# Probabilities of batch 0 turned by a trip through HBM and VectorE's block transpose, with attention three tiles behind the scores

## The chip, the cores and the metric

The kernel runs on one core of a Trainium2 chip. The metric is the device time of one launch in microseconds. TensorE is called PE in the profile, VectorE DVE, ScalarE ACT, GpSimd POOL, and SyncE, which issues most DMAs, SP. Each engine takes its instructions in order; semaphores order engines among each other.

## The reference

Two batches of 1024 tokens, width 512, all in float32.

```python
xn = layernorm(x)                                  # x: (2, 1024, 512)
q, k, v = split(xn @ w_qkv.T + b_qkv)
probs = softmax(q @ k.T / sqrt(512))               # one head, 1024 x 1024 for a batch
s = (probs @ v) @ w_out.T + b_out
logits = xn @ router_w + router_b                  # 8 experts
top2 of logits, weights = softmax(top2)
comb = sum over the top 2 of weight * silu(xn @ expert_w[e] + expert_b[e])
y = xn + comb @ proj_w + proj_b
out = x + s * silu(norm_w * y / rms(y))
```

## The kernel before

**Precision and folding.** Every product of two float32 matrices is made as three matmuls (function `product`, L1449): a value is split into a high half, as ScalarE casts it, and a low half, the difference, made by VectorE or GpSimd. Output weights are folded into the values and query weights into the keys, so that a query tile's attention is: scores (`scores`, 24 matmuls), row maximum, exp, turn of the probabilities, product with the values (`attend`, 24 matmuls), division and bias (`attn_out`).

**Stages.** Weights are folded; both batches are normalised, and their rows go to HBM (`rows_scratch`); values of batch 0; logits; then attention of batch 0, during which VectorE also works out the routing (`choose`, a generator whose steps stand between the other work), GpSimd sends every token's row into its expert's slots in HBM by indirect DMA, and ScalarE and GpSimd split expert weights; then 39 tiles of expert work; values, attention, projection and output of batch 1 and the output of batch 0.

**Attention of batch 0.** Eight tiles of 128 queries against 1024 keys, in two blocks of four. At the head of a block TensorE makes four key products (`key_weights`, 12 matmuls each), whose halves (`t_hi` on ScalarE, `t_lo` on VectorE) are the stationary side of the scores. Key products, value products, attention products and expert products share the two banks of the PSUM tensor `ab` in the order of the list `U`; each waits until the entry two before it is read (`ab_read`). Scores go to two pairs of banks (`sc`), and `scores` of a tile waits for exp of the tile two before it. `tp`, two banks, takes what is turned.

For each tile VectorE finds the maximum (`row_max`, L1245 to L1249) and ScalarE makes exp into `prob`, a single 128x1024 buffer. TensorE turns it by eight 128x128 transposes into `tp` (`turn_probs`, L1457), ScalarE copies the high half (`pt_split`, L906), VectorE the low half (`pt_low`, L1264), and TensorE makes the product. Order on TensorE in a block: scores 0 and 1, turn 0, scores 2, turn 1, product 0, scores 3, turn 2, product 1, turn 3, product 2, product 3.

**Around it.** SyncE stores each result tile of attention (L533), loads rows to be sent (L496), and, as the last tiles pass, raw weights of experts 3 and 4 (`load_raw`), biases, and the rows of the first expert tiles (`load_pair`, L502: four DMAs that bring quarters of 128 rows to 32 partitions each). VectorE turns those rows in blocks of 32x32 (`turn`, L1237), and ScalarE and VectorE split them (`g_split`, `g_low`). GpSimd loads six raw weights through two halves of a buffer (`BY_BUFFER`); ScalarE makes high halves (`early_high`, `w_high`), GpSimd low halves. The first expert tile waits for the halves of four experts (`EARLY`) and for both attention banks.

```python
                for j in range(QB):
                    if j >= 1:
                        pt_split(j - 1)
                    if (i, j) in EARLY_AT:
                        early_high(EARLY_AT.index((i, j)))
```

## Time and profile before

| | us |
|---|---|
| median of 3 runs (507.84 to 508.83) | 508.24 |
| the profiled execution | 505.39 |
| its span, first to last instruction | 503.7 |
| TensorE busy | 488.0 |
| VectorE busy | 299.7 |
| ScalarE busy | 206.7 |
| GpSimd busy | 202.6 |

The profile is of one execution. A row of a timeline has the start from the span's begin, the duration, the engine, the source line and the operation with output and inputs; in brackets stands how long the engine had been idle and what ended that. A slice of the page is 12.6 us; its digit is the busy share in tenths. Matmuls are pipelined, so their records overlap.

### The profile page before, as it was taken

Reading aid. Unit: us, or ns where it says so; the run is one execution under the profiler, and the core shown is the slowest. Engines: PE = TensorE matmul, PEld = TensorE weight load, DVE = VectorE, ACT = ScalarE, POOL = GpSimd, SP = SyncE. Lnnn points to the kernel's source line nnn. Section 1 sums busy time; section 2 is a strip of 40 time slices with the busy share of each in tenths; the row PEclk is TensorE's granted clock in tenths of the full one; section 3 lists DMA queues with packets and bytes.
Section 4 is the critical chain, followed back from the end, with each engine's and each line's share of the span. In section 5 each row is a group of like instructions: output and inputs, shape, how many; then the busy total and the mean of one; then the engine's idle time right before and its main releaser. Section 6 shows DMA issues by size and latency. Waiting matters only on the chain.

```text
span 503.7 us, 7293 instructions
## 1 busy us (share of the span) xinstructions
PE 488.0 (97%) x2234; PEld 397.2 (79%) x2235; DVE 299.7 (60%) x452; ACT 206.7 (41%) x300; POOL 202.6 (40%) x288
## 2 busy tenths in 40 slices
PE   4999999999999999799999999999999999999996
PEld 2678686888888888688888888878888888888884
DVE  2556252576422535688888889763676645667452
ACT  1166373142212333854444444323454362525550
POOL 3044310004887835860000000754477772466134
PEclk9999999999999999999999999999999999999999
DMA  7863999912688489998985666987253451331202
GB/s 261 303 231 145 379 384 366 394 43 84 220 310 298 159 248 285 307 272 247 287 219 189 188 202 181 311 287 276 65 148 114 150 175 62 116 95 62 84 33 94
DMA packets 68364, 104.22 MB, mean 207 GB/s; under 512 B 5728, under 2 KB 29808, under 8 KB 68336
## 3 DMA queue, kind: packets, MB, share of 16 engines
q1 hardware_dynamic: 55120, 67.13, 42.1%
q0 software_dynamic: 7360, 25.19, 14.6%
q10 hardware_dynamic: 5856, 11.54, 6.5%
q8 instruction: 16, 0.26, 0.2%
q14 instruction: 12, 0.10, 0.1%
HBM read 60.32 MB, written 43.52 MB: 206 GB/s over the span
## 4 chain that ended last, share of the span: by engine, by line
PE 90%; DMA 3%; issue 2%; ACT 2%; POOL 1%; DVE 1%; SPq 1%; ACTq 0%
PE ab L1451 20%; PE ab L1453 20%; PE ab L1452 20%; PE sc L1451 6%; PE sc L1453 6%; PE sc L1452 6%; PE tp L1457 4%; PE sc L1468 3%; DMA raw<-in_expert_w 2%; PE tp L1502 2%; DMA raw_o<-in_w_out_t 1%; PE sc L1531 1%; PE ab L1476 1%; ACT W L941 1%; PE sc L1534 1%
## 5 line engine op out<-in xcount | busy, mean ns | idle before, releaser
L720 POOL DMA_INDIRECT y<-y_scratch,pos x32 | 31.1, 972 | 107.2 <-DMA y_scratch<-yt_so 92.5
L1451 PE MATMUL ab<-W,st_h 128*128 x156 | 60.9, 390 | 2.7 <-DVE st_l L1189 2.7
L1453 PE MATMUL ab<-W,st_l 128*128 x156 | 60.7, 389 | 0.0
L1452 PE MATMUL ab<-W,st_h 128*128 x156 | 60.7, 389 | 0.0
L703 POOL DMA_INDIRECT rows_scratch<-xb,pos x32 | 31.2, 976 | 52.4 <-DVEq L1185 44.2
L1451 PE MATMUL sc<-xt_h,t_h 128*128 128x512 f32 x128 | 50.3, 393 | 0.0
L1453 PE MATMUL sc<-xt_h,t_l 128*128 128x512 f32 x128 | 50.0, 390 | 0.0
L1452 PE MATMUL sc<-xt_l,t_h 128*128 128x512 f32 x128 | 49.8, 389 | 0.0
L932 ACT CAST st_h<-tp 128x512 fp32r<-128x512 f32 x39 | 22.9, 588 | 42.8 <-PE ab L1453 34.1
L1245 DVE TENSOR_REDUCE small<-sc 128x1 f32<-128x1024 f32 x16 | 19.6, 1224 | 29.8 <-PE sc L1453 25.4
L1451 PEld LDWEIGHTS ab<-W,st_h 128*128 128x128 f32 x156 | 29.3, 188 | 9.6 <-issue 3.5
L1453 PEld LDWEIGHTS ab<-W,st_l 128*128 128x128 f32 x156 | 29.3, 188 | 6.1
L1452 PEld LDWEIGHTS ab<-W,st_h 128*128 128x128 f32 x156 | 29.3, 188 | 5.9
L1082 DVE SCALAR_TENSOR_TENSOR t_l<-ab,tb,t_h 128x512 fp32r<-128x512 f32 x16 | 12.0, 750 | 34.3 <-ACT t_h L832 34.3
L1189 DVE TENSOR_TENSOR st_l<-tp,st_h 128x512 fp32r<-128x512 f32 x39 | 26.5, 681 | 4.5 <-ACT st_h L932 4.4
L832 ACT ACTIVATE t_h<-ab,tb 128x512 fp32r<-128x512 f32 x16 | 11.0, 690 | 42.5 <-PE ab L1453 40.4
L1237 DVE STREAM_TRANSPOSE tp<-xn 128x512 f32<-128x512 f32 x24 | 26.3, 1098 | 3.3 <-DMA xn<-rows_scratch 1.0
L1453 PEld LDWEIGHTS sc<-xt_h,t_l 128*128 128x128 f32 x128 | 24.0, 188 | 5.0
L1452 PEld LDWEIGHTS sc<-xt_l,t_h 128*128 128x128 f32 x128 | 24.0, 188 | 4.9
L1451 PEld LDWEIGHTS sc<-xt_h,t_h 128*128 128x128 f32 x128 | 24.0, 188 | 4.8
L1237 DVE STREAM_TRANSPOSE tp<-xg 128x512 f32<-128x512 f32 x23 | 25.1, 1097 | 2.2
L1451 PE MATMUL ab<-v_h,p_h 128*128 128x512 f32 x64 | 25.6, 400 | 0.0
(261 smaller groups left out, 1219.0 us busy)
## 6 DMA issues: line engine op xcount, KB each, us to landing
rows_scratch<-xn ACTq DMA_DIRECT2D x3, 3328.0 KB, 19.3
xb<-in_expert_w POOLq DMA_DIRECT2D x6, 1024.0 KB
xn<-rows_scratch SPq DMA_DIRECT2D x48, 128.0 KB, 3.0
xg<-rows_scratch SPq DMA_DIRECT2D x44, 128.0 KB
y_scratch<-yt_own SPq DMA_DIRECT2D x20, 256.0 KB, 2.6
y_scratch<-yt_so SPq DMA_DIRECT2D x19, 256.0 KB, 2.8
rows_scratch<-xs SPq DMA_DIRECT2D x16, 256.0 KB, 6.0
xb<-rows_scratch SPq DMA_DIRECT2D x16, 256.0 KB, 6.2
```

The costliest lines, as they stand in the source:

```text
L703: pool.indirect_dma_start(slots_d, bass.IndirectOffsetOnAxis(pos[:, g:g + 1], 0), sent_rows[:, g % GB, :], None).then_inc(sent[g % GB], 16)
L720: pool.indirect_dma_start(y[:, q, :], None, y_d, bass.IndirectOffsetOnAxis(pos[:, GB * s + p:GB * s + p + 1], 0))\
L932: nc.scalar.copy(st_h[:, h, :, :], tp[:, h, :, :]).then_inc(g_hi, 1)
L1082: vec.scalar_tensor_tensor(low[:, n, :], bank(("t", b, i, n)), tb[:, n:n + 1], high[:, n, :], ALU.add, ALU.subtract).then_inc(ab_read, 1)
L1189: vec.tensor_tensor(st_l[:, h, :, :], tp[:, h, :, :], st_h[:, h, :, :], ALU.subtract).then_inc(g_lo, 1)
L1237: vec.transpose(tp[:, q % 2, :, :].rearrange("p c (r s) -> p c r s", r=4), rows[q].rearrange("p (r q c) -> p c r q", r=4, c=KC)).then_inc( ...
L1245: link(vec.tensor_reduce(small[:, at, 0:1], sc[:, n % 2, :, :], AX.XY, ALU.max, negate=True))
L1451: nc.tensor.matmul(dst, lh, rh, start=start, stop=False)
L1452: nc.tensor.matmul(dst, lh, rl, start=False, stop=False)
L1453: return nc.tensor.matmul(dst, ll, rh, start=False, stop=stop)
L1457: last = nc.tensor.transpose(tp[:, h, c, :], src[:, c * P:(c + 1) * P], ident[:, :])
L1468: last = nc.tensor.matmul(sc[:, n // 2, n % 2, :], every_fourth(raw[2][:, c, :], n), raw[3][:, c, :], start=(c == 0), stop=(c == KC - 1))
```

## The change

The turn of batch 0's probabilities leaves TensorE. Exp writes a tile with its columns in another order, so that the row falls into four quarters of 256 values. SyncE stores the tile to HBM (`p_scratch`, 512 KB) and reads it back by four DMAs of 128 KB; in the way back quarter a of all 128 rows lands in partitions 32a to 32a+31. Two block transposes on VectorE (`p_turn`) then give what the eight transposes of TensorE gave. Three tile buffers (`prob`, and `xn` or `yt_own`) hold what is being stored, and the two halves of `xs` what came back.

The two blocks become one run of eight tiles, and the product with the values follows its scores three tiles behind. The second set of key products stands behind scores 3 and product 0. The orders of SyncE, ScalarE and VectorE are written out anew; in the routing, positions now come before the table of experts (`texp`), with a semaphore for each (`routed`, `assigned`). Raw weights 3 come through the buffer on GpSimd's queue, and raw weights 6 by a DMA of ScalarE in a place of their own.

```diff
-    BY_BUFFER = EARLY + (5, 6)
+    BY_BUFFER = EARLY + (3, 5)
...
+    p_d = nc.dram_tensor("p_scratch", (GB, P, S), F32).ap()
+    p_q = p_d.rearrange("j (r s) (a f) -> j a s r f", r=4, a=4)
...
-              + [u for i in range(NB) for u in [("t", 0, i, n) for n in range(KC)]
-                 + [("a", 0, QB * i + j) for j in range(QB)]]
+              + [("t", 0, 0, n) for n in range(KC)] + [("a", 0, 0)]
+              + [("t", 0, 1, n) for n in range(KC)] + [("a", 0, j) for j in range(1, GB)]
...
+        xn_flat = xn[:, :, :].rearrange("p a n -> p (a n)")
+        yt_flat = yt_own[:, :, :].rearrange("p a n -> p (a n)")
+        probs = tuple(prob[:, :] if j % 2 == 0 else xn_flat if j < QB else yt_flat for j in range(GB))
+        quarters = tuple(xs[:, 2 * n:2 * n + 2, :].rearrange("p a n -> p (a n)") for n in range(2))
...
-            sb("experts_0_to_2", [P, 3, 2, KC, D], F32R, a)
-            sb("expert_3_high", [P, KC, D], F32R, a)
-            raw_3 = sb("raw_3", [P, KC, D], F32, a)
+            sb("experts_0_to_3", [P, 4, 2, KC, D], F32R, a)
             sb("expert_4_high", [P, KC, D], F32R, a)
             raw_4 = sb("raw_4", [P, KC, D], F32, a)
-            sb("experts_5_to_7", [P, 3, 2, KC, D], F32R, a)
+            sb("expert_5", [P, 2, KC, D], F32R, a)
+            sb("expert_6_high", [P, KC, D], F32R, a)
+            raw_6 = sb("raw_6", [P, KC, D], F32, a)
...
-            for j in range(GB):
-                if j == QB + 1:
-                    sp.wait_ge(s_done, GB)
-                    load_raw(sp, 3)
-                    load_bias(0)
-                    load_bias(1)
-                if j == QB + 2:
-                    sp.wait_ge(ptr_done, 1 + GB)
-                    load_pair(2, 1)
-                    load_raw(sp, 4)
-                    load_next(4, 0)
-                    load_bias(2)
-                    load_bias(3)
...
+            def store_prob(j):
+                sp.wait_ge(exp_done, 2 + j + 1)
+                sp.dma_start(p_d[j], probs[j], max_dma_last_dim=4 * D).then_inc(p_out[j % 2], 16)
+            def load_prob(j):
+                sp.wait_ge(p_out[j % 2], 16 * (j // 2 + 1))
+                if j >= 2:
+                    sp.wait_ge(p_turned, j - 1)
+                for a in range(4):
+                    sp.dma_start(quarters[j % 2][32 * a:32 * (a + 1), :].rearrange("p (r f) -> p r f", r=4),
+                                 p_q[j, a, :, :, :]).then_inc(p_in[j % 2], 16)
+            def store_s(j):
                 sp.wait_ge(ab_read, 2 + U["a", 0, j] + 1)
                 sp.dma_start(s_g[j], so[:, j % 2, :]).then_inc(so_st[j % 2], 16)
-                if 1 <= j <= 3:
-                    for g in range(GB + 3 * j - 3, min(GB + 3 * j, G)):
-                        load_to_send(g)
-                if j == QB:
-                    for g in range(GB):
-                        sp.wait_ge(sent[g], 64)
-                    load_pair(0, 0)
-                if j == QB + 3:
-                    load_next(6, 1)
-                    for k in range(4, E):
-                        load_bias(k)
+            sp.wait_ge(t_done, G)
+            for j in range(QB):
+                store_prob(j)
+                load_prob(j)
+            store_s(0)
+            for g in range(GB, GB + 4):
+                load_to_send(g)
+            for j in (QB, QB + 1):
+                store_prob(j)
+                load_prob(j)
+                store_s(j - 3)
+                for g in range(GB + 4 + 2 * (j - QB), GB + 6 + 2 * (j - QB)):
+                    load_to_send(g)
+            store_prob(GB - 2)
+            load_prob(GB - 2)
+            store_s(3)
+            store_prob(GB - 1)
+            load_prob(GB - 1)
+            sp.wait_ge(s_done, GB)
+            load_raw(sp, 4)
+            for g in range(GB):
+                sp.wait_ge(sent[g], 64)
+            load_pair(0, 0)
+            store_s(4)
+            load_pair(2, 1)
+            load_bias(0)
+            load_bias(1)
+            store_s(5)
+            load_next(4, 0)
+            load_bias(2)
+            load_bias(3)
+            store_s(6)
+            store_s(7)
+            load_next(6, 1)
...
-                    act.wait_ge(routed, 1)
+                    act.wait_ge(assigned, 1)
...
-            def attention_block(i):
-                for c in range(KC):
-                    if i or c:
-                        t_hi(0, i, c)
-                def pt_split(j):
-                    act.wait_ge(ptr_done, 1 + QB * i + j + 1)
-                    nc.scalar.copy(pt_h[:, j % 2, :, :], tp[:, :, :, :].rearrange("p a c n -> p (a c) n"))\
-                        .then_inc(pt_hi, 1)
-                for j in range(QB):
-                    if j >= 1:
-                        pt_split(j - 1)
-                    if (i, j) in EARLY_AT:
-                        early_high(EARLY_AT.index((i, j)))
-                    act.wait_ge(mx, QB * i + j + 1)
-                    act.wait_ge(ptr_done, QB * i + j + 1)
-                    nc.scalar.activation(prob[:, :], sc[:, j % 2, :, :].rearrange("p a n -> p (a n)"), ACT.Exp,
-                                         bias=small[:, 4 + j, 1:2], scale=SCALE,
-                                         accum_out=small[:, 4 + j, 2:3]).then_inc(exp_done, 1)
-                    if i == 0 and j == 0:
-                        act.wait_ge(gate_d, 1)
-                        nc.scalar.activation(small[:, 10, :], small[:, 9, :], ACT.Exp).then_inc(gate_e, 1)
-                pt_split(QB - 1)
...
+            def pt_split(j):
+                act.wait_ge(p_turned, j + 1)
+                if j >= 2:
+                    act.wait_ge(ab_full, U["a", 0, j - 2] + 1)
+                nc.scalar.copy(pt_h[:, j % 2, :, :], tp[:, :, :, :].rearrange("p a c n -> p (a c) n")).then_inc(pt_hi, 1)
+            def exp_0(j):
+                act.wait_ge(mx, j + 1)
+                if j >= 2:
+                    act.wait_ge(p_out[j % 2], 16 * (j // 2))
+                nc.scalar.activation(probs[j].rearrange("p (a c q) -> p c a q", a=4, q=32),
+                                     sc[:, j % 2, :, :].rearrange("p m (c a q) -> p (m c) a q", a=4, q=32), ACT.Exp,
+                                     bias=small[:, 4 + j % QB, 1:2], scale=SCALE,
+                                     accum_out=small[:, 4 + j % QB, 2:3]).then_inc(exp_done, 1)
+            for n in range(1, KC):
+                t_hi(0, 0, n)
+            exp_0(0)
+            act.wait_ge(gate_d, 1)
+            nc.scalar.activation(small[:, 10, :], small[:, 9, :], ACT.Exp).then_inc(gate_e, 1)
+            act.wait_ge(zero_in, 48)
+            exp_0(1)
+            early_high(0)
+            pt_split(0)
+            exp_0(2)
+            exp_0(3)
+            pt_split(1)
+            pt_split(2)
+            for n in range(KC):
+                t_hi(0, 1, n)
+            early_high(1)
+            exp_0(4)
+            pt_split(3)
+            exp_0(5)
+            early_high(2)
+            pt_split(4)
+            exp_0(6)
+            pt_split(5)
+            exp_0(7)
+            pt_split(6)
+            early_high(3)
+            act.wait_ge(s_done, GB)
+            w_high(0)
+            w_high(1)
+            pt_split(7)
...
+            w_high(2)
+            w_high(3)
...
-            load_raw(act, E)
+            load_raw(act, 6)
...
-                row_max(QB * i)
-                go_on()
-                row_max(QB * i + 1)
-                go_on()
-                pt_low(0)
-                row_max(QB * i + 2)
-                go_on()
-                pt_low(1)
-                go_on()
-                attn_out(0)
-                row_max(QB * i + 3)
-                pt_low(2)
-                attn_out(1)
-                pt_low(3)
-                if tail:
-                    dve.wait_ge(pt_lo, 1 + GB)
-                    turn(0, 0, 0, True)
-                    turn(1, 1, 0, True)
-                    g_low(0, 0)
-                    g_low(1, 1)
-                attn_out(2)
-                attn_out(3)
-                if tail:
-                    turn(2, 2, 0)
-                    turn(3, 3, 0)
...
+            def p_turn(j):
+                dve.wait_ge(p_in[j % 2], 64 * (j // 2 + 1))
+                dve.wait_ge(pt_lo, j)
+                back = quarters[j % 2].rearrange("p (r c q) -> p c r q", r=4, q=32)
+                for h in range(2):
+                    last = vec.transpose(tp[:, h, :, :].rearrange("p c (r s) -> p c r s", r=4),
+                                         back[:, h * KC:(h + 1) * KC, :, :])
+                last.then_inc(p_turned, 1)
...
+            routing = choose()
+            for n in range(KC):
+                t_lo(0, 0, n)
+                if n == 2:
+                    read_logits()
+            next(routing)
+            row_max(0)
+            next(routing)
+            row_max(1)
+            next(routing)
+            p_turn(0)
+            row_max(2)
+            pt_low(0)
+            next(routing)
+            next(routing, None)
+            row_max(3)
+            p_turn(1)
+            pt_low(1)
+            p_turn(2)
+            attn_out(0)
+            pt_low(2)
+            p_turn(3)
+            for n in range(KC):
+                t_lo(0, 1, n)
+            for j in range(3, GB - 1):
+                row_max(j + 1)
+                attn_out(j - 2)
+                pt_low(j)
+                p_turn(j + 1)
+            attn_out(GB - 3)
+            pt_low(GB - 1)
+            dve.wait_ge(pt_lo, GB)
+            turn(0, 0, 0, True)
+            turn(1, 1, 0, True)
+            g_low(0, 0)
+            g_low(1, 1)
+            attn_out(GB - 2)
+            attn_out(GB - 1)
+            turn(2, 2, 0)
+            turn(3, 3, 0)
...
-                def turn_probs(j):
-                    a = QB * i + j
-                    pe.wait_ge(exp_done, a + 3)
-                    pe.wait_ge(pt_lo, a + 1)
-                    transpose_tile(prob[:, 0:KC * P], 0)
-                    transpose_tile(prob[:, KC * P:2 * KC * P], 1).then_inc(ptr_done, 1)
-                def attend_tile(j):
-                    pe.wait_ge(pt_lo, QB * i + j + 2)
-                    attend(0, QB * i + j, pt_h[:, j % 2, :, :], pt_l[:, j % 2, :, :], v_h, v_l)
-                if not route_here:
-                    for n in range(KC):
-                        key_weights(0, i, n)
-                scores(0, QB * i)
-                if route_here:
-                    count_chosen()
-                scores(0, QB * i + 1)
-                pe.wait_ge(lg_read, 1)
-                if route_here:
-                    pe.wait_ge(cnt_read, 1)
-                turn_probs(0)
-                scores(0, QB * i + 2)
-                turn_probs(1)
-                attend_tile(0)
-                scores(0, QB * i + 3)
-                turn_probs(2)
-                attend_tile(1)
-                turn_probs(3)
-                attend_tile(2)
-                attend_tile(3)
...
+            def attend_tile(j):
+                pe.wait_ge(pt_lo, j + 1)
+                attend(0, j, pt_h[:, j % 2, :, :], pt_l[:, j % 2, :, :], v_h, v_l)
+            scores(0, 0)
+            count_chosen()
+            for j in range(1, QB):
+                scores(0, j)
+            attend_tile(0)
+            for n in range(KC):
+                key_weights(0, 1, n)
+            for j in range(QB, GB):
+                scores(0, j)
+                attend_tile(j - 3)
+            for j in range(GB - 3, GB):
+                attend_tile(j)
...
-            pe.wait_ge(routed, 1)
+            pe.wait_ge(assigned, 1)
```

`w_high` is as before and only moved up; `pt_low` and `attn_out` are as before but for their index.

## Rows read from the trace of the kernel before

**Rows 1.** The page: busy time by engine, DMA share and rate by slice

```profile
PE 488.0 (97%) x2234; PEld 397.2 (79%) x2235; DVE 299.7 (60%) x452; ACT 206.7 (41%) x300; POOL 202.6 (40%) x288
...
DMA  7863999912688489998985666987253451331202
GB/s 261 303 231 145 379 384 366 394 43 84 220 310 298 159 248 285 307 272 247 287 219 189 188 202 181 311 287 276 65 148 114 150 175 62 116 95 62 84 33 94
```

**Rows 2.** Timeline of PE at the first expert tiles (start us, us, what)

```profile
199.85 0.39 PE L1451 MATMUL ab<-W,st_h 128*128 x1
...
205.07 0.39 PE L1453 MATMUL ab<-W,st_l 128*128 x1
207.80 0.49 PE L1451 MATMUL ab<-W,st_h 128*128 x1 [2.35 <-DVE st_l L1189]
...
211.17 0.49 PE L1451 MATMUL ab<-W,st_h 128*128 x1 [0.36 <-DVE st_l L1189]
```

**Rows 3.** Timeline of PE, scores of tile 1 and the transposes behind them

```profile
99.95 0.48 PE L1451 MATMUL sc<-xt_h,t_h 128*128 128x512 f32 x1
...
105.51 1.04 PE L1457 MATMUL tp<-ident,prob 128*128 128x128 f32 x8
```

**Rows 4.** The chain that ended last, the same eight transposes

```profile
105.68 0.88 PE tp L1457 x8
```

**Rows 5.** Timeline of DVE, two block transposes of expert rows and two low halves

```profile
191.43 2.06 DVE L1237 STREAM_TRANSPOSE tp<-xn 128x512 f32<-128x512 f32 x2
193.40 1.44 DVE L1189 TENSOR_TENSOR st_l<-tp,st_h 128x512 fp32r<-128x512 f32 x2
```

**Rows 6.** Timeline of DVE in the attention of batch 0

```profile
100.25 1.22 DVE L1245 TENSOR_REDUCE small<-sc 128x1 f32<-128x1024 f32 x1
...
105.79 1.22 DVE L1245 TENSOR_REDUCE small<-sc 128x1 f32<-128x1024 f32 x1 [1.45 <-PE sc L1453]
...
107.37 0.17 DVE L1152 COPY w<-small 128x16 f32<-128x16 f32 x1
...
109.73 1.23 DVE L1264 TENSOR_TENSOR pt_l<-tp,pt_h 128x1024 fp32r<-128x1024 f32 x1
...
113.66 0.47 DVE L1171 TENSOR_TENSOR slots<-slot_i,small 128x312 f32<-128x312 f32 x1
...
114.90 1.23 DVE L1264 TENSOR_TENSOR pt_l<-tp,pt_h 128x1024 fp32r<-128x1024 f32 x1
116.04 0.28 DVE L1178 SCALAR_TENSOR_TENSOR route<-small,route 128x128 f32<-128x128 f32 x1
...
118.51 0.17 DVE L1270 RECIPROCAL small<-small 128x1 f32<-128x1 f32 x1 [0.15 <-PE ab L1453]
118.71 0.75 DVE L1272 SCALAR_TENSOR_TENSOR so<-ab,small,sbias 128x512 f32<-128x512 f32 x1
```

**Rows 7.** Timeline of ACT, attention and first expert tiles

```profile
102.96 0.19 ACT L917 ACTIVATION_READ_ACCUMULATOR prob<-sc,small 128x1 f32 x1
...
106.59 1.01 ACT L906 CAST pt_h<-tp 128x1024 fp32r<-128x1024 f32 x1 [3.33 <-PE tp L1457]
...
192.61 0.59 ACT L932 CAST st_h<-tp 128x512 fp32r<-128x512 f32 x1 [2.47 <-DVE tp L1237]
...
194.01 2.00 ACT L941 CAST W<-raw 128x1024 fp32r<-128x1024 f32 x2
```

**Rows 8.** Stores of expert outputs (L548, 256 KB each), 225 to 300 us

```profile
DMA to landing us min/median/max: 2.0/2.6/4.5
```

**Rows 9.** Loads of expert rows (L502, 128 KB each), 225 to 300 us

```profile
DMA to landing us min/median/max: 2.4/2.7/4.5
```

**Rows 10.** Timeline of SyncE's queue, four loads of expert rows

```profile
217.14 1.82 SPq L502 DMA_DIRECT2D xg<-rows_scratch  x4
```

**Rows 11.** DMA issues, 128 to 140 us (size each, us to landing)

```profile
xb<-rows_scratch SPq DMA_DIRECT2D x4, 256.0 KB, 4.1
```

**Rows 12.** DMA issues of the whole span, the raw expert weights

```profile
raw<-in_expert_w SPq DMA_DIRECT2D x2, 1024.0 KB, 9.3
```

88 lines of the change are left out of this document (37 added, 51 removed).

## The prediction

> **What bounds the kernel now.** The page's busy line comes first: TensorE (PE) is busy in 97% of the span [rows 1], so what TensorE sheds is worth its full time as long as nothing takes its place, and every stall put on it costs in full. The DMA and GB/s lines under it say where the queues are full: digits 1 and 2 from 101 to 126 us, 6 to 8 up to 164, 4 up to 176, 8 or 9 behind that. PE's timeline shows how the matmuls follow each other: 24 of them (one tile's scores, or one tile's attention product) from 199.85 take 5.45 us, 0.227 each [rows 2]. The records are 0.39 long because they overlap; the distance between starts is what counts. The same rows hold the only idle PE between the start of batch 0's attention and the end of the experts: 2.35 and 0.36 us at the third and fourth expert tile, both ended by st_l. The fourth starts at 211.17; three tiles back (12 matmuls, 2.72 us each) that is 203.0. A kernel whose expert tiles ran without a gap would equal this one if its first started at 203.0, not 199.85. I use that as the mark.
>
> **Removed.** Eight 128x128 transposes for each of 8 tiles. PE's timeline has a group of eight at 105.51 [rows 3]; the chain that ended last charges such a group 0.88 us [rows 4]. Eight groups are 7.1 us. All of it lies on the bound, so with no new wait the first expert tile would start at 199.85 - 7.1 = 192.75.
>
> **Added on VectorE.** Two block transposes for a tile. The trace has the operation in the same form into the same PSUM tensor: two take 2.06 us, about 2.0 up to the next [rows 5]; 8 tiles are 16 us on an engine that has room on average (60%). But its queue is in order, and where a turn stands in it decides. The transposed copy waits for data out of HBM, and row_max of the next tile stands behind it.
>
> **Early: VectorE's queue.** Only rows of before, and the new order. Scores 1 start at 99.95 [rows 3] and scores 3 end at 116.4 (three tiles, the first 0.1 longer, no transposes). VectorE's durations up to its next operation, from [rows 6]: row_max 1.58; routing step three 2.36; the low half of the probabilities 1.14; slots and texp 1.24; positions 2.47; attn_out 0.95. From row_max's start to the end of exp, with its read of the sum, are 2.9 us (100.25 to 103.15 [rows 6, 7]). The turn of tile 0 needs its round trip through HBM: exp 0 ends at 103.15, and with 7.5 us for the trip (below) the quarters are there at 110.7. From there: turn 0 to 112.7, row_max 2 to 114.3, low half 0 to 115.45 (so the attention product of tile 0 starts at 116.4 unhindered), positions to 117.9, texp to 119.15, row_max 3 to 120.75, turn 1 to 122.75, 1.3 us until ScalarE has its high half (1.0 us [rows 7] and two hand-overs), low half 1 to 125.2, turn 2 to 127.2, attn_out 0 to 128.15. TensorE wants that bank long before: product 0 ends at 121.9, key product 0 at 124.6, and key product 1 writes the bank that attn_out 0 reads. Stall: 128.3 - 124.6 = 3.7 us. Key product 2 needs the first t_lo, which now stands behind low half 2 (to 129.55) and turn 3: exp 3 ended at 122.1, plus 7.5 is 129.6, turned at 131.6, t_lo (0.75, as any 128x512 of this kind) at 132.3. TensorE is ready at 131.0: 1.4 us more. Together 5.1 us, nearly all of it VectorE's own work and little of it DMA. In the old order the same t_lo found VectorE idle. Scores 4 start at 132.75 + 5.1 = 137.85.
>
> **Late: a loop through HBM.** For tiles 4 to 7 the queue reads row_max, attn_out, low half, turn of the same tile. So exp of tile j, its store, its load, its turn and then row_max of tile j+1 form one ring. Its period is D + 2.0 (turn) + 2.9 (row_max and exp) = D + 4.9, where D is the time from the end of exp to the quarters' arrival. TensorE's own period is scores plus product, 10.9 us. The ring is slower than TensorE once D exceeds 6.0, and the three tiles of lag hide that only until the scores run out. In numbers: scores 4 end at 143.3, exp 4 ends at 146.4, exp 7 at 146.4 + 3(D + 4.9) = 161.1 + 3D, and product 7 can start D + 2.0 + 2.6 later (turn, high half, low half, hand-overs): 165.7 + 4D. TensorE is ready for it at 137.85 + 10 x 5.45 = 192.35.
>
> **D**, from both sides. A 512 KB store, then four loads of 128 KB. In the expert stage 256 KB stores land 2.0 at least and 2.6 us in the median after issue, 128 KB loads 2.4 and 2.7 [rows 8, 9]. Another 256 KB at 394 GB/s, the highest of the page's slices [rows 1], is 0.67. Four issues take 1.82 us on SyncE's queue, the fourth starting about 1.4 after the first [rows 10]. Below: 2.0 + 0.67 + 0.1 + 1.4 + 2.4 = 6.6. Medians: 2.6 + 0.67 + 0.1 + 1.4 + 2.7 = 7.5, which I take for tiles 0 to 3, where the queues are nearly empty (digits 1 and 2 [rows 1]). Above: in the attention stage itself, beside the rows being sent, a 256 KB load took 4.1 [rows 11]; with 4.1 for both kinds and slower issues D = 4.1 + 0.67 + 0.1 + 1.8 + 4.1 = 10.8. Tiles 4 and 5 travel among the sends (digit 8), tile 7 beside a 1 MB weight load (digit 8 again). For the mean of tiles 4 to 7 I take 8.4, nearer to the medians since tile 6 falls where the digit is 4. Then product 7 starts at 199.3, a stall of 7.0 us.
>
> The page "DMA: Bandwidth & Descriptors" of the Trainium skill (section "Anatomy of one DMA") gives a DMA 2.0 us fixed plus its bytes at 436 GB/s, and names HBM as the heaviest target for the receipt; it was fitted on GpSimd's path. By it the store is 3.2 and a load 2.3, and an estimate of D is 3.2 + 0.1 + 1.4 + 2.3 = 7.0. The stores' 2.6 agrees with it; the 4.1 does not.
>
> **Into the experts.** SyncE loads raw_4 only behind the loads of tile 7: 161.1 + 3D + 0.1 + 3.3 + 1.8. It lands 9.3 later [rows 12]; ScalarE makes two high halves of it (2.0 [rows 7]), only then splits the first two expert tiles (0.6 each), then VectorE's g_low (0.7 [rows 5]) and attn_out 6 (0.95), 0.25 hand-overs. The first expert tile can start at 180.7 + 3D = 205.9, or, by product 7, at 171.15 + 4D = 204.75. The later decides: 205.9, a further 1.1 us. In return the old gaps at the third and fourth expert tile (3.15 us by the mark) go, because raw_4 is now converted before them. The sends start some 0.3 us earlier and lose about 2 us where GpSimd waits for the second high half (now behind t_hi); neither is late for anything up to tile 7. All else (layout of the raw weights, biases) lies under TensorE's work. Batch 1 is unchanged.
>
> **Sum.** -7.1 + 5.1 + 7.0 + 1.1 - 3.15 = +2.9, and by the mark, 205.9 - 203.0 = +2.9. That is against the profiled execution (505.39, span 503.7). The median of the runs is 508.24, 2.9 above it; I add the difference to the median: 511.1.
>
> **Rivals.**
> A. Short round trip, faster. One quantity decides: start of the experts is 180.7 + 3D, so the break-even is D = 7.4. At 7.0 it is 201.7 (-1.3, 506.9), at 6.6 200.5 (-2.5, 505.7). For it: stores that landed in 2.0 us; the queues have spare time between sends. Against it: the 4.1 us. This is also where the page's fixed cost would put it. Faster by over 1.0 us needs D below 7.1. Chance 0.17.
> B. D between 7.1 and 7.7: within 1 us of no change. Chance 0.17.
> C. Contention: D near 10.8 for all four. Product 7's path takes over: 171.15 + 43.2 = 214.35, +11.3, 519.6. For it: the digit 8 in the stretches of tiles 4, 5 and 7 [rows 1], and 1 MB more is added to each tile. Against it: sends pause while GpSimd makes low halves. D from 9.5 up, chance 0.13.
> D. All waits are hidden and only the removal shows: -7.1 - 3.15, 498.0. It would need VectorE to be through 5 us sooner in the early part, for which no row speaks. Chance 0.03.
>
> **Chances and range.** My forecast (D from 7.7 to 9.5; +0.8 to +6.2) has 0.50. A measurement of this kernel can tell 0.2%, 1 us, from no change: faster 0.20 (A, D), same 0.17 (B), slower 0.63. The range reaches from A's lower end to C's: 505.5 to 519; the forecast's own is 509 to 514.5.
>
> **What would show it.** No wait of TensorE on st_l at the third expert tile. A stall of 3 to 5 us ahead of the second key product of queries 4 to 7, ended by attn_out (so), and a smaller one ahead of the third, ended by t_l. VectorE's turns of tiles 5 to 7 waiting for quarters, and row_max starting right after a turn, later than its scores ended. A TensorE stall of some 7 us ahead of the last product, ended by pt_l. The forecast falls if the round trip is under 7.1 us or the turn stands elsewhere on VectorE than I read; if the stall at the key products is missing, it is my sum of VectorE's queue that is wrong.

## The result, and the profile after

| | median us | range | runs | ratio to before, 95% interval |
|---|---|---|---|---|
| before | 507.84 | 505.47 to 508.83 | 5 | |
| after | 522.31 | 521.26 to 524.91 | 5 | 1.0289 (1.0257 to 1.032) |

The change makes the kernel 2.9% slower, some 14.5 us. The prediction had the sign right and the size wrong: 511.1, with a range that ended at 519. The profiled execution of after took 524.91, the slowest of its runs, with a span of 523.1 against 503.7: +19.4. Some 5 us of that are those two executions and not the kernels: the profiled one of before lies 2.5 us under its median, that of after 2.6 us above. Traces below are compared with that span, kernels by their ratio to before on the same chip (before's median differs by up to 3.4 us from chip to chip).

The page of the kernel after: PE has 64 instructions fewer (2170 for 2234), the eight groups of eight transposes. Its share falls from 97% [rows 1] to 94%, and the clock digits, all 9 before behind the first, fall to 8 and 7:

```profile
PE 493.4 (94%) x2170; PEld 397.9 (76%) x2171; DVE 308.2 (59%) x468; ACT 206.6 (39%) x300; POOL 202.1 (39%) x288
...
PEclk9999999999899998897999999999999999999999
DMA  8764999966749869995997666699323641242202
...
PE 68%; DMA 16%; DVE 7%; issue 3%; SPq 2%; ACT 1%; POOL 1%; DVEq 0%; ACTq 0%
```

The last line is the chain that ended last, by engine. A sixth of it is now DMA: between 147 and 236 us PE no longer sets the pace.

PE's timeline at the key products of queries 4 to 7 (their normal distance is the 0.227 of [rows 2]):

```profile
124.89 0.39 PE L1521 MATMUL ab<-xt_h,mw 128*128 128x512 f32 x1
128.18 0.50 PE L1519 MATMUL ab<-xt_h,mw 128*128 128x512 f32 x1 [2.90 <-DVE so L1329]
...
129.16 0.63 PE L1519 MATMUL ab<-xt_h,mw 128*128 128x512 f32 x1
129.59 0.63 PE L1520 MATMUL ab<-xt_l,mw 128*128 128x512 f32 x1
...
132.40 0.40 PE L1521 MATMUL ab<-xt_h,mw 128*128 128x512 f32 x1
134.72 0.50 PE L1519 MATMUL ab<-xt_h,mw 128*128 128x512 f32 x1 [1.93 <-DVE t_l L1139]
```

These are the two early stalls that were predicted, and for the predicted reasons: attn_out 0, then the first t_lo. From start to start they cost 3.29 and 2.32 us, 3.06 and 2.09 over the pace of 0.227: together 5.15 against 5.1. What was not predicted stands between them: starts 0.43 apart, not 0.227. The granted clock of such stretches (a row has the window, its length, PE's busy time with its matmuls, the granted clock, the DMA share, GB/s):

```profile
125.00:140.00 15.00, 10.17 (x30) 0.77 0.89 298
142.00:188.00 46.00, 46.00 (x205) 1.00 0.74 260
190.00:201.00 11.00, 7.69 (x22) 0.69 0.61 202
210.00:217.00 7.00, 4.68 (x13) 0.76 1.09 292
```

Before, the windows from 95 to 500 us all have 1.00. Here the clock falls from 2.4 to 1.2 GHz for some 3 to 6 us behind five stalls, of 2.1 to 3.8 us. The Trainium skill, "TensorE: Matmul & The Clock Gate" (section "What's actually happening"), states that this gate knows only full and half clock; the two distances of 0.227 and 0.43 agree with it.

The chain from tile 4 on (start, us, what), the ring that was predicted:

```profile
147.54 1.24 DVE small L1303
...
151.22 3.12 DMA p_scratch<-prob
...
155.71 3.94 DMA xs<-p_scratch
159.66 1.32 DVE tp L1315 x2
160.98 1.10 DVE small L1303
162.58 0.99 issue
163.78 6.43 DMA p_scratch<-yt_own
...
171.56 4.23 DMA xs<-p_scratch
175.81 1.32 DVE tp L1315 x2
177.13 1.11 DVE small L1303
```

Row_max, exp, store, load, turn, row_max: the maximum of the next tile (L1303) starts right behind each turn. Four ends of exp (151.19, 163.76, 179.91, 192.12) give a period of 13.64; D + 4.9 with D = 8.4 had given 13.3. D itself was 8.5, 12.05, 8.1 and 7.2, mean 8.96, and 7.4 for tile 0, where 7.5 was taken; the turn is 1.32 and not 2.0. The three periods hold the first three of these trips, with a mean of 9.5, and all else in a period takes 4.1, not 4.9.

The predicted stall of 7.0 us ahead of the last product stands elsewhere: PE waits 3.5 us ahead of product 6 (190.63 to 194.33), whose high half stands behind exp 7 in ScalarE's queue, then loses 3.0 us at half rate, and product 7 itself waits only 0.2. The same chain at its way into the experts, and PE's stalls there:

```profile
192.14 2.75 DMA p_scratch<-yt_own
...
196.69 0.43 SPq L408
...
199.42 7.00 DMA xn<-rows_scratch
206.51 2.10 DVE tp L1295 x2
...
210.09 10.30 DMA xn<-rows_scratch
...
222.12 11.00 DMA raw_p<-in_proj_w
...
234.09 0.59 ACT st_h L994
234.71 0.70 DVE st_l L1247
```

```profile
211.04 0.79 PE L1519 MATMUL ab<-W,st_h 128*128 x1 [2.33 <-DVE so L1329]
...
216.73 0.49 PE L1519 MATMUL ab<-W,st_h 128*128 x1 [1.28 <-DVE so L1329]
...
228.88 0.50 PE L1519 MATMUL ab<-W,st_h 128*128 x1 [0.32 <-DVE st_l L1247]
...
235.54 0.79 PE L1519 MATMUL ab<-W,st_h 128*128 x1 [3.63 <-DVE st_l L1247]
```

The old gaps at the third and fourth tile [rows 2] are gone (0.3 us lost at each), but others stand at the first, second, sixth and seventh. A DMA of 128 KB that took 2.4 to 4.5 us in [rows 9] takes 7.0 and 10.3 here; and a 1 MB load of raw_p holds ScalarE, behind which a tile's split stands.

**Where the 16.5 us beyond the predicted 2.9 lie.** The first expert tile starts at 211.04, predicted 205.9: 5.1 late. From there to the end are 312.06 us; before, without its gaps, 300.7 (503.7 - 203.0). So 11.4 more are lost behind the first expert tile, where the prediction had nothing. 10.9 of them lie at the expert tiles (117.1 us for the 39 tiles, 106.2 before without its gaps): stalls of 5.7 (1.44, 0.47 and 3.79 over the pace) and some 5.2 of slow spacing. The rest of the span is 0.5 longer. The 5.1 ahead of it: scores 4 end at 147.54 instead of 143.3 (+4.2), exp 4 follows 0.5 later than reckoned, three periods are 1.0 longer, and the way from exp 7 to the first expert tile is 18.9, reckoned 19.6. That last number is right by luck, since the way is another: raw_4 landed after 7.5 us, not 9.3, and what came last were the expert rows asked for behind it, which the sum left out.

### The profile page after: what moved, and what is told of

Same layout as the page of the kernel before. It is cut to its first block, busy times and chain, and to the rows that moved or that the text cites. A ratio compares the mean times of both kernels' runs of the same rounds, so it can differ in the third digit from the quotient of the medians.

```text
span 523.1 us, 7229 instructions
## 1 busy us (share of the span) xinstructions
PE 493.4 (94%) x2170; PEld 397.9 (76%) x2171; DVE 308.2 (59%) x468; ACT 206.6 (39%) x300; POOL 202.1 (39%) x288
## 4 chain that ended last, share of the span: by engine, by line
PE 68%; DMA 16%; DVE 7%; issue 3%; SPq 2%; ACT 1%; POOL 1%; DVEq 0%; ACTq 0%
PE ab L1519 16%; PE ab L1520 16%; PE ab L1521 16%; DMA xs<-p_scratch 4%; PE sc L1519 4%; PE sc L1521 4%; PE sc L1520 4%; DMA xn<-rows_scratch 3%; PE sc L1535 3%; PE tp L1525 3%; DMA raw_p<-in_proj_w 2%; DMA p_scratch<-yt_own 2%; DMA p_scratch<-prob 2%; PE tp L1569 2%; DVE small L1303 2%
## 5 line engine op out<-in xcount | busy, mean ns | idle before, releaser
L1519 PE MATMUL ab<-W,st_h 128*128 x156 | 63.4, 406 | 7.6 <-DVE st_l L1247 3.9
L1520 PE MATMUL ab<-W,st_h 128*128 x156 | 62.3, 400 | 0.0
L1521 PE MATMUL ab<-W,st_l 128*128 x156 | 62.2, 399 | 0.0
L1519 PEld LDWEIGHTS ab<-W,st_h 128*128 128x128 f32 x156 | 30.4, 195 | 16.4 <-issue 10.1
L1520 PEld LDWEIGHTS ab<-W,st_h 128*128 128x128 f32 x156 | 30.5, 195 | 6.2
L1519 PE MATMUL ab<-xt_h,mw 128*128 128x512 f32 x64 | 26.7, 418 | 4.8 <-DVE so L1329 2.9
L1519 PE MATMUL ab<-v_h,pt_h 128*128 128x512 f32 x64 | 26.4, 413 | 3.4 <-DVE pt_l L1321 3.3
L1303 DVE TENSOR_REDUCE small<-sc 128x1 f32<-128x1024 f32 x16 | 19.4, 1214 | 14.8 <-PE sc L1521 14.6
L730 POOL TENSOR_TENSOR W<-xb,W 128x512 fp32r<-128x512 f32 x16 | 20.5, 1291 | 17.4 <-ACT W L935 17.1
## 6 DMA issues: line engine op xcount, KB each, us to landing
rows_scratch<-xn ACTq DMA_DIRECT2D x3, 3328.0 KB, 19.4
xb<-in_expert_w POOLq DMA_DIRECT2D x6, 1024.0 KB, 10.3
```

Source lines behind the costliest of these rows:

```text
L730: pool.tensor_tensor(W[:, e, 1, c, :], wraw[:, k % 2, c, :], W[:, e, 0, c, :], ALU.subtract).then_inc(e_lo, 1)
L1303: link(vec.tensor_reduce(small[:, at, 0:1], sc[:, n % 2, :, :], AX.XY, ALU.max, negate=True))
L1519: nc.tensor.matmul(dst, lh, rh, start=start, stop=False)
L1520: nc.tensor.matmul(dst, lh, rl, start=False, stop=False)
L1521: return nc.tensor.matmul(dst, ll, rh, start=False, stop=stop)
```

## The experiments

Two theories stood first. **Clock**: the half-rate stretches, 11 us of PE's pace in all, are what was missed. **Queue order**: the waits of the ring and the entry are, and slow stretches lie beside them. A third, **bytes**, came in with the second group. Kernels that ran on different chips are compared by the ratio; where medians are used it is said. Short diffs are against the kernel after unless said otherwise.

**filled**: 68 matmuls on operands that lie there anyway, into a bank nobody reads at the time, put into the stalls.

```diff
+            pe.wait_ge(exp_done, 2 + 3)
+            fill(13)
             key_weights(0, 1, 1)
+            fill(9)
```

> The changed kernel with 68 extra matmuls whose result nobody reads, put where TensorE stood still: 13 and 9 ahead of the second and third key product of queries 4 to 7, 14 ahead of product 6, 10, 6 and 16 ahead of expert tiles 0, 1 and 6. They are work added, nothing else moves. Theory 1 (each stall lowers the granted clock, and matmuls behind it start 0.43 us apart, not 0.23, which costs 11 us in all): the granted clock reads 1.00 nearly everywhere, the slow stretches go, and the time falls by 7 to 11 us, to 512 to 515. Theory 2 (the wide spacing comes from contention for memory while transfers and turns are busy, or the stalls alone explain the loss): spacing stays at 0.43, the time stays at 522 or rises by up to 3 us where a filler outlasts its stall.

521.49 us, ratio 1.0268 (1.0231 to 1.0304). Two windows of this kernel show the clock restored:

```profile
125.00:140.00 15.00, 13.80 (x60) 1.00 0.89 297
...
229.00:242.00 13.00, 12.80 (x57) 1.00 0.86 228
```

The first expert tile starts at 211.18 as before (211.04), though scores 4 end 2.2 us sooner (145.31): the ring and the entry had slack for the slow matmuls. What had been slow clock ahead of product 7 is now a wait: it stalls 2.9 us for pt_l, and behind this stall, which no fill covers, the granted clock is 0.79 (201 to 209 us). Behind the first expert tile the rest is 306.6 long, 5.4 shorter in this profile; the medians differ by 1 us only, within both intervals. The clock theory of 7 to 11 us fell, and so did the other, since the spacing was mended; what the clock costs at the end lies between 0 and 5.

**turn_at_once**: VectorE turns out of exp's buffer; stores and loads are still issued. (ScalarE and SyncE get one more wait on the turns each, so that no buffer is overwritten too soon; these two lines aren't shown.)

```diff
-                dve.wait_ge(p_in[j % 2], 64 * (j // 2 + 1))
+                dve.wait_ge(exp_done, 2 + j + 1)
...
-                back = quarters[j % 2].rearrange("p (r c q) -> p c r q", r=4, q=32)
+                back = probs[j].rearrange("p (r c q) -> p c r q", r=4, q=32)
```

> The changed kernel, but VectorE's turn reads the tile that exp wrote and waits for exp alone; all stores and loads of probabilities are still issued and move the same bytes. It leaves out the exchange of quarters, so the products use other numbers. Theory 1 (the trip sits in the ring exp, trip, turn, row_max of the next tile, and in the last tiles delays exp 7 by 10 us): row_max starts with the end of its scores, product 6 finds its halves ready, the loads of raw weights 4 and expert rows leave SyncE some 6 us sooner, and the time is 510 to 515. The stall ahead of the second key product stays (over 2.5 us), since that is VectorE's own queue. Theory 2 (the loss is transfers that crowd each other, or VectorE's turns): the bytes are the same, so the time stays within 3 us of 522.

518.72, ratio 1.0193 (1.0135 to 1.0252). The ring is broken (exp 7 ends at 179.56, 12.6 us sooner), yet the first expert tile comes only 3.2 sooner, at 207.89: VectorE waits 7.90 us there for xn, whose loads were asked for at 187.6. Waiting in the ring is 1%, where theory 1 had 1.4 to 2.4%; the rest is elsewhere.

**early_order** and **ring_order** move VectorE's and ScalarE's instructions only.

```diff
             p_turn(1)
+            attn_out(0)
             pt_low(1)
+            t_lo(0, 1, 0)
             p_turn(2)
-            attn_out(0)
```

> The changed kernel, with VectorE's attn_out 0 moved ahead of low half 1 and the t_lo of the second set of keys put between turns 2 and 3 as they fall due (ScalarE's t_hi 0 ahead of high half 2). Theory 1 (two stalls of 3.1 and 2.1 us and 3.3 us of slow clock behind them come from the place of attn_out and t_lo in VectorE's queue): both stalls vanish and scores 4 start 8 us sooner. Of that about 2 to 8 us reach the end, since the ring through HBM starts sooner too: 514 to 520. Theory 2 (the key products wait for the trip of tile 3, not for the queue): the third key product still waits, and the time is 521 to 523.

518.66, ratio 1.0189 (1.0138 to 1.024). The two early stalls are gone (0.3 us left) and scores 4 end at 139.7, 7.8 sooner; product 6 stalls 6.8 instead of 3.5, and the first expert tile is at 206.44, 4.6 sooner.

```diff
+            row_max(QB)
             for j in range(3, GB - 1):
-                row_max(j + 1)
                 attn_out(j - 2)
                 pt_low(j)
+                if j + 2 < GB:
+                    row_max(j + 2)
                 p_turn(j + 1)
```

> The changed kernel, with VectorE's row_max of the next tile put ahead of the turn in tiles 4 to 7; nothing else. Theory 1 (row_max behind the turn makes each exp wait for the trip of the tile before it, four times over): row_max 5 to 7 start within 0.5 us of the end of their scores, exp 7 ends near 188 us instead of 192, no stall ahead of product 6, and the time falls by 4 to 8 us to 514 to 518. Theory 2 (the trips are late for TensorE whatever the order, since the three tiles of lag are too short for them): product 6 or 7 still stalls and the time is 520 to 523.

516.5, ratio 1.0191 (1.0135 to 1.0246). Exp 7 ends at 180.09 and the first expert tile starts at 200.84: 10.2 us sooner in the profile, though behind it 10.1 more than the gapless 300.7 are again lost (stalls of 1.5, 1.2 and 3.8, slow spacing). Both parts of the predicted mechanism are there, and each is worth some 1% (two chips, intervals of 0.3 to 0.6% to either side).

**sends_free** puts the second early_high ahead of exp 3, so that GpSimd doesn't wait for it (7.8 us in after, at 144.7).

> The changed kernel with one instruction of ScalarE moved: the high half of the second expert's weights (early_high 1) stands ahead of exp 3 instead of behind the second set of t_hi. Theory 1 (that place holds GpSimd for 7.8 us, so the sends end 6 to 8 us later than before, meet the trips of tiles 5 and 6, and keep SyncE from loading the first expert rows): the sends end near 177 us instead of 183, and the time falls by 1 to 4 us. Theory 2 (the sends are hidden anyway, since SyncE reaches the expert rows only behind the trip of tile 7): the sends end earlier and the time stays within 1 us of 522.

521.31, ratio 1.0296 (1.0249 to 1.0344). Nothing. The edit did only part of what it was for: GpSimd then stood 3.2 and 3.6 us for rows to send, and the sends ended at 181.0, 2.1 us sooner, not 6 (183.1 in after, 175.5 in before). That they are late for nobody, as the prediction had it, fits the trace of after, where the rows of the experts are asked for at 197.4 only; the wait itself was four times as long as put down.

**entry_order** asks for raw_4 and the first rows ahead of the trip of tile 7, **all_orders** joins the early and ring orders with raw_4 ahead of that trip and the rows behind it (its lines are shown). Both also ask for raw_p right behind raw_6.

```diff
             store_s(3)
-            store_prob(GB - 1)
-            load_prob(GB - 1)
-
             sp.wait_ge(s_done, GB)
             load_raw(sp, 4)
+            store_prob(GB - 1)
+            load_prob(GB - 1)
```

> The changed kernel with SyncE's and ScalarE's DMAs at the entry of the experts moved: raw weights 4 and the first pair of expert rows are issued ahead of the trip of tile 7, the store of result tile 5 ahead of the second pair, and the projection's raw weights right behind raw weights 6. Theory 1 (once the last product is due, late transfers in SyncE's queue and one late load on ScalarE set the pace: 2.5, 1.4 and 3.8 us of stalls at expert tiles 0, 1 and 6): these three stalls shrink below 1 us each and the time falls by 5 to 9 us, to 513 to 517. Theory 2 (the stalls come from full queues, so an earlier issue lands no earlier): the time stays within 2 us of 522.

> The order changes together: attn_out and t_lo early, row_max ahead of the turn, and the DMAs of the entry moved (the first pair of expert rows stays behind the trip of tile 7, raw weights 4 go ahead of it). Trip and turn stay as they are. Theory 1 (the loss is where the new work stands in four queues, not the work itself): no stall over 1 us is left in the attention, and the time is 500 to 507, at or below the kernel before. Theory 2 (the trip itself is the loss: 8 MB more to move among the sends and weights): 510 or more is left.

entry_order: 524.71, ratio 1.0407 (1.0354 to 1.046), with single runs from 517.47 to 527.62. all_orders: 512.36, 1.0131 (1.0087 to 1.0176). Neither came near its first theory. **all_and_sends**, which adds the edit of sends_free to all_orders and was expected 1 to 4 us below it, took 513.01, ratio 1.0177 (1.0106 to 1.0248): no gain. The loads moved ahead are paid for by the trip behind them. DMA issues of all_orders, 170 to 195 us (size, us to landing):

```profile
xb<-in_expert_w POOLq DMA_DIRECT2D x2, 1024.0 KB, 9.2
...
raw<-in_expert_w SPq DMA_DIRECT2D x1, 1024.0 KB, 10.2
...
p_scratch<-yt_own SPq DMA_DIRECT2D x1, 512.0 KB, 12.7
```

The 512 KB store took 12.7 us with 2 MB of weights in flight beside it; five stores of after took 2.7 to 3.1.

**trip_first** is all_orders with raw_4 left behind the trip; **raw_p_early** is after with raw_p asked for right behind raw_6.

> Edit: the early order of VectorE, row_max ahead of the turn, store_s(5) ahead of load_pair(2, 1), and raw_p asked for right behind raw_6, all as in all_orders; but the 1 MB raw_4 load stays behind the trip of tile 7, as in the changed kernel. Theory 1 (the order in the queues: in all_orders the trip of tile 7 took 12.7 us because its store shared the engines with the 1 MB load ahead of it): trip 7 is back at 7 to 9 us, the stall ahead of product 7 falls from 8.6 to under 3 us, the first expert tile starts at 197 to 200, and the time is 505 to 509 (ratio 0.998 to 1.005). Rival (bytes: what must be moved before the experts is the same in any order, so what the trip wins raw_4 and the first rows lose): the first expert tile stays at 203 or later, and the time is 511 to 514 (ratio 1.010 to 1.016).

> Edit: the changed kernel with one line moved: ScalarE asks for raw_p right behind raw_6, not behind the second expert tile's split. Theory 1 (ScalarE's conversion of raw_p, due at once, holds back the split of the expert tile behind it): the stall of 3.8 us at the seventh expert tile goes, nothing ahead of it changes (first expert tile at 210.5 to 212), the time is 517.5 to 519.5 (ratio 1.020 to 1.024). Rival (another 1 MB in flight beside the first rows moves the stall to them): the first or second expert tile starts 2 to 4 us later, and the time is 521 to 524, no gain (ratio 1.027 to 1.033).

trip_first: 511.68, ratio 1.0059 (1.003 to 1.0087), the best of those with all eight trips. Trip 7 took 12.4 us (177.04 to 189.47), its store 5.0: neither the hoped-for 7 to 9 nor the 17 of all_orders. The first expert tile is at 200.33, between the two theories. VectorE's timeline shows what is left:

```profile
169.47 1.32 DVE L1315 STREAM_TRANSPOSE tp<-xs 128x512 f32<-128x512 f32 x2 [6.35 <-DMA xs<-p_scratch]
...
189.47 1.32 DVE L1315 STREAM_TRANSPOSE tp<-xs 128x512 f32<-128x512 f32 x2 [6.26 <-DMA xs<-p_scratch]
```

The turn of tile 5 starts 16.0 us after its exp ended (153.47). D of tiles 4 to 7 is 9.6, 16.0, 15.2 and 13.0, mean 13.5, where after had 8.96: with the orders mended, the sooner exp is ready the longer the trip takes, and D is no constant. raw_p_early: 520.02, 1.0231 (1.0197 to 1.0265). The stall of 3.8 at the seventh tile is gone, but one of 3.4 stands at the fourth, where VectorE waits 3.9 us for expert rows, much as the rival had it. The intervals of the two ratios overlap, so what the place of raw_p is worth isn't shown.

**Bytes or SyncE's queue.** no_trip leaves the stores and loads out of turn_at_once. no_queue keeps them, but the loads read the input, so SyncE doesn't stand behind the stores.

```diff
                 if j >= 2:
                     sp.wait_ge(p_turned, j - 1)
-                                 p_q[j, a, :, :, :]).then_inc(p_in[j % 2], 16)
+                                 x_8[j, a // 2, a % 2, :, :, :]).then_inc(p_in[j % 2], 16)
```

> Edit: the changed kernel with its own orders, but VectorE turns each tile straight out of the buffer that exp wrote, and the stores and loads of probabilities are left out (in turn_at_once they were still issued, with nobody waiting). Rows are then not exchanged between partition quarters, so the probabilities that reach the product are in a wrong order; every other operation is kept. Theory 1 (what the trip costs beside its wait is its place in SyncE's queue and its bytes, which delay raw_4 and the first rows of the experts): the stall of 5.0 us at the first expert tile goes, the first expert tile starts at 200 to 204, the time is 511 to 515 (ratio 1.006 to 1.014), 4 to 7 us below turn_at_once (518.7). Rival (the bytes cost nothing, the order of VectorE and ScalarE is what is left): within 1.5 us of turn_at_once, 517 to 520 (ratio 1.018 to 1.026).

> Edit: as turn_at_once (VectorE turns out of exp's buffer, nobody waits for the probabilities), but the four 128 KB loads read the input x, in pieces of the same size, so SyncE no longer waits for a store before it asks for them. Bytes and DMAs are those of the change, the stops of SyncE's queue are gone (probabilities reach the product in a wrong order). turn_at_once took 518.7 (ratio 1.0193), no_trip 509.4 (1.0029). Theory 1 (the 9 us between them are bytes that share the DMA engines with sends and weights): 516 to 520, ratio 1.014 to 1.023. Rival (they are SyncE's queue, which stands behind each store for some 3 us and asks for everything else late): 509 to 513, ratio 1.002 to 1.009.

no_trip: 509.38, ratio 1.0029 (1.0004 to 1.0053). no_queue: 514.92, 1.0191 (1.016 to 1.0221), the same as turn_at_once. The windows from 150 to 200 us of turn_at_once, no_queue and no_trip:

```profile
150.00:200.00 50.00, 46.87 (x201) 0.97 0.97 312
```

```profile
150.00:200.00 50.00, 48.80 (x215) 1.00 0.99 319
```

```profile
150.00:200.00 50.00, 50.00 (x222) 1.00 0.88 275
```

With the trips the DMA engines are busy 0.97 and 0.99 of that time (0.78 in before), and what is in flight there lands late. In the kernel after itself the same window has only 0.80, since there each trip waits for the one before. The turn of the first expert rows in no_queue and no_trip:

```profile
199.16 2.08 DVE L1302 STREAM_TRANSPOSE tp<-xn 128x512 f32<-128x512 f32 x2 [4.92 <-DMA xn<-rows_scratch]
```

```profile
190.51 2.13 DVE L1287 STREAM_TRANSPOSE tp<-xn 128x512 f32<-128x512 f32 x2
```

So in these kernels, where nobody waits for the probabilities, the bytes cost 1.6%, 8 us (the three ran on three chips; by the medians it is 5.5 to 9.3), and SyncE's stops nothing that can be measured. The first expert tile, at 207.89 and 203.69 with the bytes, starts at 197.81 without them. Yet behind it no_trip still takes 308.2 us, 7.5 more than the gapless 300.7: ScalarE waits there 2.7 us for raw_6 and 4.9 for raw_p, with a tile's split behind each, and PE stalls 1.3 and 4.1. Of the 11.4 us that after loses in that stretch most are thus there without a byte of the trips. The Trainium skill, "DMA: Bandwidth & Descriptors" (section "Issuing engines are not separate DMA queues"), says that DMAs of SyncE, ScalarE and GpSimd run on the same 16 engines and interleave there; these runs agree with it: another order of asking moved the wait and didn't remove it.

**no_trip_orders** is trip_first without stores and loads.

> Edit: trip_first with the stores and loads of probabilities left out as in no_trip (probabilities then reach the product in a wrong order). It is the change with its eight groups of transposes gone, VectorE's turns kept and well placed, and no trip. Theory 1 (all that is lost comes from the trip and from the orders): no stall over 1.5 us up to the product of tile 7, the first expert tile at 193 to 195, a time of 498 to 501 (ratio 0.982 to 0.990), and 5 to 9 us below trip_first. Rival (the entry into the experts is bound by its own loads and conversions whatever the trip does): the first expert tile at 198 or later with the stall moved there, 503 to 508 (ratio 0.993 to 1.003).

503.97, ratio 0.9931 (0.9899 to 0.9962), in the range of the rival. It is 7.7 us below trip_first on the same chip, which is what the trips, waits and bytes together, cost there. Even so only 3.5 us are gained where 7.1 + 3.15 had been shed: stalls of 0.7 and 0.9 are left in the attention and 1.9 and 2.8 in the experts (first expert tile at 195.21). The old gaps move, they don't vanish, though no trip is left.

**Which trips are worth it.** four_trips turns tiles 4 to 7 on TensorE again (early order of trip_first), eight_by_tensor all of them.

```diff
+            def turn_late(j):
+                pe.wait_ge(exp_done, 2 + j + 1)
+                pe.wait_ge(pt_lo, j)
+                transpose_tile(probs[j][:, 0:KC * P], 0)
+                transpose_tile(probs[j][:, KC * P:2 * KC * P], 1).then_inc(p_turned, 1)
             for j in range(QB, GB):
                 scores(0, j)
+                if j > QB:
+                    turn_late(j - 1)
                 attend_tile(j - 3)
```

> Edit: orders of trip_first, but only tiles 0 to 3 go through HBM and VectorE; tiles 4 to 7 are turned by TensorE's transposes as before (tile j behind scores j+1), exp writes them in the plain order. It computes the reference. Theory 1 (the trips cost where the DMA engines are full, from tile 4 on, and are free in tiles 0 to 3): four groups of transposes saved (-3.5), the old gaps at the expert tiles gone (-3.15), some 2 us of gaps at other expert tiles: first expert tile at 196 to 199, 502 to 506, ratio 0.988 to 0.997, faster than the kernel before. Rival (the entry into the experts is bound by its own loads, as the first two stalls in no_trip_orders hint): first expert tile at 199 or later, 507 to 511, ratio 0.998 to 1.006.

> Edit: four_trips with tiles 0 to 3 turned by TensorE too, so nothing passes through HBM and what is left of the change is its order (three tiles of lag, raw weights moved, early order of VectorE). It computes the reference. Theory 1 (tiles 0 to 3 go through HBM free of charge): 3.5 us above four_trips, 505 to 509, ratio 0.995 to 1.002. Rival (the trips of tiles 0 to 3 or VectorE's turns cost there what the transposes cost): within 1 us of four_trips or below it.

four_trips: 504.7, ratio 0.9988 (0.9961 to 1.0015); from 95 us to the experts PE stalls 0.5 us only, and the first expert tile is at 197.09. eight_by_tensor: 514.28, 1.0178 (1.0138 to 1.0217), which tells nothing of the transposes: in my order they stood where the bank `tp` was still unread, two stalls of 3.2 and 2.4 us and 4 us of slow spacing. Three more kernels mended that and moved raw_p to a later place.

```diff
-                if 1 <= i < 5:
-                    w_high(i + 5)
-                if i == 1:
-                    load_raw(act, E)
+                if i in (1, 2):
+                    w_high(i + 5)
+                if i == 2:
+                    load_raw(act, E)
+                if i in (6, 7):
+                    w_high(i + 2)
```

> Edit: four_trips, but raw_p is asked for at the third expert tile (not ahead of the first) and ScalarE makes its high halves at the seventh and eighth tile (not the fourth and fifth). It computes the reference. In four_trips the rows for the sixth expert tile were asked for at 200.3 and landed 12.5 us later, right behind raw_6 (197.3) and raw_p (197.7), 1 MB each; a stall of 3.5 us at that tile followed. Theory 1 (bytes ahead of the rows): the stall falls under 1.5 us, 501.5 to 504.5 where before is at 505.3, ratio 0.992 to 0.998. Rival (ScalarE's queue or raw_6 alone is what holds the rows up): the stall stays over 2.5 us, ratio 0.998 or more.

> Edit: four_late_p with tiles 0 to 3 turned by TensorE too, and, other than in eight_by_tensor, with VectorE's low halves 0 and 1 ahead of the row maxima 2 and 3 and ScalarE's high half 1 ahead of exp 3, so that the tile before is out of the bank when TensorE comes to turn the next. It computes the reference. In eight_by_tensor two stalls of 3.2 and 2.4 us ahead of transposes (TensorE waiting until the low half before was read) and 4 us of slow spacing behind them hid what the transposes themselves cost. Theory 1 (tiles 0 to 3 go through HBM and VectorE free of charge): no stall over 1 us in the attention, 3 to 4.5 us above four_late_p, ratio 0.998 to 1.005. Rival (the early trips cost as much as the transposes save): within 1 us of four_late_p.

> Edit: trip_first (all eight tiles through HBM) with raw_p late as in four_late_p. It computes the reference. Theory 1 (bytes): the stall of 3.9 us at the expert tile at 215 falls under 1.5 us, ratio 0.999 to 1.003 (trip_first 1.0059). Rival: it stays, ratio 1.004 to 1.008. In both the distance to four_late_p is what the trips of tiles 4 to 7 cost over TensorE's four groups of transposes: by theory 1 4 us or more (stall ahead of product 7 of 4 us, slow spacing of up to 5 us, less 3.5 saved).

| | trips | median us | ratio to before, 95% interval |
|---|---|---|---|
| trip_late_p | 8 | 511.73 | 1.0129 (1.0097 to 1.0161) |
| four_late_p | 4 | 503.4 | 0.9972 (0.9951 to 0.9992) |
| eight_late_p | 0 | 509.62 | 1.0094 (1.0065 to 1.0124) |

In nearly the same orders and on one chip, the trips of tiles 0 to 3 gain 1.2% over TensorE's transposes (6 us, of which four groups of 0.88 are 3.5; the rest are a stall of 1.1, slow spacing and what follows), and those of tiles 4 to 7 lose 1.6% (0.7% by trip_first against four_trips). trip_late_p has the median of trip_first (511.73 and 511.68), from which it differs only in raw_p's place, but a ratio 0.7% higher, since before's median is 3.4 us lower on its chip. Either raw_p's late place costs 0.7% or ratios from two chips agree only to that much; no run tells which. four_late_p is faster than both kernels, by 0.3% over before, an interval that just leaves out 1.

eight_late_p was expected at 0.998 to 1.005 and missed it. It makes all eight groups of transposes as before and has no trip, and is 0.9% slower than before: what is left of the change, the lag, the orders and the moved raw weights, costs about that much by itself. Its first expert tile starts at 200.33, 0.5 later than before's; behind it stand stalls of 2.3 and 2.9 us.

In four_trips the largest stall, 3.5 us, was at the sixth expert tile, where VectorE waited for rows:

```profile
212.86 1.09 DVE L1298 STREAM_TRANSPOSE tp<-xg 128x512 f32<-128x512 f32 x1 [4.04 <-DMA xg<-rows_scratch]
```

In four_late_p it is gone, as the theory of the bytes ahead of these rows had it. But nothing is gained: the fifth tile now stalls 3.2 us (1.0 in four_trips) and the eighth 2.1. ScalarE's timeline of four_late_p at the fifth:

```profile
197.11 0.39 ACTq L408 DMA_DIRECT2D raw<-in_expert_w  x1
...
208.55 1.04 ACT L936 CAST W<-raw 128x1024 fp32r<-128x1024 f32 x1 [4.53 <-DMA raw<-in_expert_w]
```

It is raw_6, asked for only when the last product ends, for which ScalarE waits with a tile's split behind it; it took 11.4 us to land, 9.3 in four_trips. That the stall would go if raw_6 were asked for sooner was not tried.

## Why the prediction was wrong in size

**Removal, -7.1: right.** The eight groups are gone (64 instructions) and nothing of the kind took their place on PE.

**Early stalls, 3.7 + 1.4: right**, in place and cause, and early_order takes them away. That 3.06 + 2.09 come to nearly the same sum is in part luck. The turn was mis-sized (1.32 for 2.0), which made up for some of a longer trip of tile 3 (9.2 for 7.5), and the half clock brought TensorE 1.7 us later to the second stall.

**The ring, period D + 4.9, D = 8.4: right as a mechanism**; ring_order and turn_at_once break it. The period (13.64 for 13.3) fits by two errors that cancel: 9.5 for 8.4 in the three trips, 4.1 for 4.9 in the rest. It began 4.2 us late, since scores 4 ended late: 3.4 of that is slow spacing behind the two early stalls, of which filled gave back 2.2. The place of exp 7 ahead of the high half of tile 6 on ScalarE wasn't reckoned; product 6, not 7, stood for it.

**"In return the old gaps at the third and fourth expert tile (3.15 us by the mark) go" and "All else (layout of the raw weights, biases) lies under TensorE's work": these are the steps that failed.** As a number, the way from exp 7 to the first expert tile fitted, 18.9 for 19.6. But the sum ended there: it took everything behind the first expert tile as gapless, and 11.4 us were lost there. The two old gaps did go, and others came. The kernel after and its variants (filled apart) all have stalls at the expert tiles behind the first, 2.2 us (entry_order) to 6.9 (ring_order), with or without trips: 3.9 in trip_first, 4.5 in four_trips, 5.4 in no_trip, 5.2 in eight_late_p. Most of those that were followed back end at expert rows, whose 128 KB loads landed after 7 to 12 us, or at ScalarE, which waits for raw_6 or raw_p with a tile's split behind it. In before ScalarE asked for raw_p at 202.56 and didn't wait for it; in after it asked at 222.12, waited 4.3 us, and TensorE stalled 3.8. The layout of the raw weights was put at nothing and isn't; how the 11.4 divide between it, the late rows and the clock stays open, because no run took the new layout out.

**Bytes were priced in one place only.** Contention was put into D (rival C: D near 10.8), where it was mild in after (8.96) but not in trip_first (13.5). Some 8 us by turn_at_once and no_queue against no_trip fall on the weights and rows that must be there when the experts begin; the rows that warned were the digits 6 to 8 from 126 us on and the 9.3 us of a raw load [rows 1, 12]. How much of after's own loss this is wasn't measured: behind the first expert tile no_trip loses 7.5 of the same 11.4.

**The clock was left out.** Stalls were priced at their length. In the trace half-rate stretches add 11 us to PE's pace; at the end they are worth 0 to 5. Of the 11.4 some 5.2 are slow spacing by the trace of after, and filled's profile gives 5.4 back, but its median only 1; which of the two holds stays open.

**The chances.** Slower at 0.63 was right. Rival C came nearest in time (519.6) for another reason than the one it named: its condition, D from 9.5 up, wasn't met by the mean of the four trips.

## What to carry to other kernels

When an engine is relieved by traffic through HBM, price the bytes against what else must land before the next stage, not only the latency of the new trip: where the DMA engines were nearly full, the added megabytes delayed what was loaded next, and three other orders of asking moved that wait without removing it. Move only the tiles that travel where the queues are empty: here the first four trips gained and the last four lost. A sum should run to the end of the span, past the stage in which the change lies. A load that a change moves is a term of it, and a gap may be struck off only when what it waited for comes sooner.
